# A pre-norm decoder layer on one core: z and h transposed by DMA instead of on TensorE, v and the cross attention as whole 128x128 products

## The reference

```python
x = x + attn(layernorm(x))            # causal, 16 heads of 16, W_qkv (768x256), W_out (256x256)
x = x + xattn(layernorm(x), ctx, mask)  # scores = q.ctx^T / 16, masked, softmax, times ctx
x = x + ffn(layernorm(x))

# ffn: two bit_linear layers round activations to 8 bits and weights to -1, 0, 1
def bit_linear(x, w, g):
    xn = x * rsqrt(mean(x * x) + 1e-5) * g
    s  = 127 / clip(max(abs(xn)), 1e-5);  xq = clip(round(xn * s), -128, 127) / s
    m  = 1 / clip(mean(abs(w)), 1e-5);    wq = clip(round(w * m), -1, 1) / m
    return xq @ wq.T
y = bit_linear(x, gate_w, gate_norm_w)        # 256 -> 1408
h = silu(y[:, :704]) * y[:, 704:]
out = bit_linear(h, down_w, down_norm_w)      # 704 -> 256
```

## Time and profile before

| | |
|---|---|
| time, median of 3 runs | 211.85 us (211.42 to 215.0) |
| the profiled execution | span 212.7 us from first to last instruction, 10882 instructions; no other time of it is given |
| busy share of the span | PE 91%, VectorE 78%, ScalarE 71%, GpSimd 64% |
| until the loop on PE begins | about 57 us |
| the loop, ten steps | about 57 to 169 us, 22.4 us for a turn of two steps |
| behind it | about 169 to 212.7 us |

### The profile page before, as it was taken

How to read it: one execution, slowest core, us unless ns; L and a number is a source line. 1 busy time by engine, 2 the same in 40 slices (tenths; PEclk the granted TensorE clock), 3 DMA queues, 4 the chain that set the end, 5 groups by cost and what they waited for, 6 DMA issues and landing times.

```text
span 212.7 us, 10882 instructions
## 1 busy us (share of the span) xinstructions
PE 194.6 (91%) x4104; PEld 153.5 (72%) x4107; DVE 165.7 (78%) x523; ACT 150.6 (71%) x422; POOL 137.1 (64%) x290
## 2 busy tenths in 40 slices
PE   4997999999999989999899989998999999889874
PEld 4785987978787868887787868787887866445532
DVE  1222587999988968798788888888879799999771
ACT  3468467767788886969587959887868866775821
POOL 4600341776758773948495857685755889999990
PEclk9998799999999999999999999999999999999999
DMA  5999000101010102020202011110101012000011
GB/s 172 379 330 348 25 3 6 52 3 51 6 49 30 53 6 74 0 76 2 76 0 74 2 28 48 32 44 25 51 25 51 24 52 77 0 5 26 2 43 59
DMA packets 11474, 12.79 MB, mean 60 GB/s; under 512 B 1009, under 2 KB 10801, under 8 KB 11442
## 3 DMA queue, kind: packets, MB, share of 16 engines
q1 hardware_dynamic: 11442, 12.41, 18.2%
HBM read 10.31 MB, written 2.10 MB: 58 GB/s over the span
## 4 chain that ended last, share of the span: by engine, by line
PE 72%; issue 10%; POOL 9%; DVE 4%; ACT 3%; DMA 1%; POOLq 0%; SPq 0%; DVEq 0%; ACTq 0%
PE ps L331 14%; PE ps L309 8%; PE ps L343 7%; PE ps L315 6%; PE ps L419 6%; PE ps L434 5%; PE ps L398 5%; PE ps L367 4%; PE ps L505 3%; PE ps L463 3%; POOL zh L1994 2%; PE ps L360 2%; PE ps L452 2%; PE ps L522 2%; PE ps L458 2%
## 5 line engine op out<-in xcount | busy, mean ns | idle before, releaser
L1994 POOL TENSOR_TENSOR zh<-hh,gd 128x352 f32<-128x352 f32 x32 | 31.2, 986 | 5.1 <-DVE hh L1331 4.7
L331 PE MATMUL ps<-yaT,wqk 128*128 128x128 f32 x256 | 32.9, 284 | 0.5 <-ACT yaT L681 0.5
L331 PEld LDWEIGHTS ps<-yaT,wqk 128*128 128x128 f32 x256 | 31.2, 199 | 1.2 <-ACT yaT L681 0.7
L1203 DVE TENSOR_REDUCE mx<-ps 128x16 f32<-128x1024 f32 x16 | 19.6, 1224 | 7.8 <-PE ps L367 7.6
L315 PE MATMUL ps<-wg,zT 128*128 128x352 bf16 x128 | 22.3, 312 | 0.5 <-ACT hT L681 0.4
L2016 POOL TENSOR_SCALAR hq<-zh,qh 128x704 f32<-128x704 f32 x16 | 13.6, 851 | 13.3 <-DVE qh L1360 13.0
L1910 POOL TENSOR_TENSOR rs<-ve,neghalf 128x1 f32<-128x1 f32 x32 | 20.2, 632 | 2.7
L681 ACT ACTIVATE hT<-ps 128x256 bf16<-128x256 bf16 (+1 forms) x32 | 15.5, 495 | 6.6 <-PE ps L309 6.5
L786 ACT ACTIVATE th_sb<-ps,th 128x352 f32<-128x352 f32 x32 | 17.4, 553 | 3.5 <-PE ps L315 1.8
L1318 DVE SCALAR_TENSOR_TENSOR th_sb<-th_sb,ps 128x352 f32<-128x352 f32 x32 | 16.4, 513 | 4.1 <-ACT th_sb L786 4.1
L738 ACT ACTIVATE pT<-ps 128x512 f32<-128x512 f32 x32 | 17.8, 609 | 1.3 <-PE ps L404 0.8
(11 more groups left out here) (120 smaller groups left out, 518.5 us busy)
## 6 DMA issues: line engine op xcount, KB each, us to landing
ct_in<-ctx_t SPq DMA_DIRECT2D x16, 128.0 KB, 2.1
cn_in<-ctx_n SPq DMA_DIRECT2D x16, 128.0 KB, 2.2
out<-o_out SPq DMA_DIRECT2D x16, 128.0 KB, 1.7
wg<-gate_t SPq DMA_DIRECT2D x1, 1408.0 KB, 7.7
x_in<-x SPq DMA_DIRECT2D x1, 1024.0 KB, 10.9
wd<-down_t SPq DMA_DIRECT2D x1, 640.0 KB, 8.7
wqk<-wqkv_t SPq DMA_DIRECT2D x1, 512.0 KB, 4.0
x_in<-x SPq DMA_DIRECT2D x1, 512.0 KB, 9.5
```

Of the source, the lines that this page charges most:

```text
L331: last = pe.matmul(qk_ps[:, e * P:(e + 1) * P], wqk[:, c, e * P:(e + 1) * P], yaT[:, t % 2, c, :], start=(c == 0), stop=(c == DC - 1))
L1203: V.tensor_reduce(out=mx[:, t % 2, :, 0, :], in_=scores, op=ALU.max, axis=AX).then_inc(ev["mx_d"], 1)
L1994: G.tensor_tensor(zh[:, t % 2, part], hh[:, t % 2, part], gd[:, part], ALU.mult).then_inc(ev[f"zh_d{j}"], 1)
```

## The change

v is projected by two products of 128x128 by 128x256, and ACT sorts the result into place with four copies instead of two. The cross attention scores of both sequences are made as one 128x128 block; the mask becomes two rows, one for each sequence, that also rule out the other sequence's 64 columns, and its product comes last instead of first. The weights `px` then need no 64x64 pieces: one transpose and one copy.

`zb` and `hb` are no longer transposed on PE: SP issues a transposing DMA from SBUF to SBUF for each, `zT` is its target and `hT` likewise, and `keep_zT`, `keep_hT_0`, `keep_hT_1` are gone from ACT. Rounding on POOL and bf16 on DVE stay as they are.

On PE the step now begins with `scores_q(s)` instead of ending with `scores_q(s+1)`; the mask part of the scores (`late_bf`) no longer waits for q and k; `scores_k` waits for the maxima only ahead of its last part; many waits for freed buffers are gone. The lists of all engines are in another order, and the first loads too. `keep_busy` has other counts: 16 ahead of `gate_up(14)`, 24 between `down(13)` and `down(14)`.

```diff
+            def transpose_z(t):                       # on SyncE
+                sp.wait_ge(ev["zb_d"], t + 1)
+                after(sp, ev["gu_ps0"], t - 1)
+                after(sp, ev["gu_ps1"], t - 1)
+                sp.dma_start_transpose(zT[:, t % 2, :, :], zb[:, t % 2, :]).then_inc(zT_ld[t % 2], 16)
+
+            def transpose_h(t):                       # on SyncE
+                sp.wait_ge(ev["hb_d"], t + 1)
...
+                after(sp, ev["d_ps"], t - 1)
+                sp.dma_start_transpose(hT[:, t % 2, :, :], hb[:, t % 2, :]).then_inc(hT_ld[t % 2], 16)
...
-                for b in range(2):                    # project_v
-                    for c in range(DC):
-                        for j in range(2):
-                            last = pe.matmul(v_ps[SEQ * j:SEQ * (j + 1), b * P:(b + 1) * P], yaT[:, t % 2, c, b * SEQ:(b + 1) * SEQ],
-                                             wv[:, c, j * P:(j + 1) * P], start=(c == 0), stop=(c == DC - 1))
+                for c in range(DC):
+                    last = pe.matmul(v_ps[:, :], yaT[:, t % 2, c, :], wv[:, c, :], start=(c == 0), stop=(c == DC - 1))
...
-                for rows in seqs:                     # cross_scores
-                    pe.matmul(sx_ps[rows, :], row_bf, mask_bf[:, t % 2, rows], start=True, stop=False)
-                for c in range(DC):
-                    for rows in seqs:
-                        last = pe.matmul(sx_ps[rows, :], yxT[:, t % 2, c, rows], ct_in[:, t % 2, c, rows], start=False, stop=(c == DC - 1))
+                for c in range(DC):
+                    pe.matmul(sx_ps, yxT[:, t % 2, c, :], ct_in[:, t % 2, c, :], start=(c == 0), stop=False)
+                pe.wait_ge(ev["mask_d"], at(t + 1))
+                pe.matmul(sx_ps, row_bf, mask_bf[:, t % 2, :], start=False, stop=True).then_inc(ev["sx_ps"], 1)
...
-                pe.wait_ge(ev["zT_d"], at(t + 1))     # gate_up_0, gate_up_1
+                pe.wait_ge(zT_ld[t % 2], loads(t, 16))
...
-                pe.wait_ge(ev["hT_d0"], at(t + 1))    # down
-                pe.wait_ge(ev["hT_d1"], at(t + 1))
+                pe.wait_ge(hT_ld[t % 2], loads(t, 16))
...
-                for j in range(2):                    # keep_v
-                    rows = slice(SEQ * j, SEQ * (j + 1))
-                    last = copy(v2[rows, t % 2, :, :, j, 0:DK], v_ps[rows, :].rearrange("p (b i d) -> p b i d", b=2, i=PAIRS))
+                for b in range(2):
+                    for j in range(2):
+                        last = copy(v2[SEQ * j:SEQ * (j + 1), t % 2, b, :, j, 0:DK],
+                                    v_ps[SEQ * b:SEQ * (b + 1), j * P:(j + 1) * P].rearrange("p (i d) -> p i d", i=PAIRS))
```

More of the change, by code:

```diff
@@ L282, in at, with loads @@
                 return kept[t.base]
-            def loads(t):
-                return 32 * (t // 2 + 1) if isinstance(t, int) else pe.snap(t.turn * 32 + 32 * (t.base // 2 + 1))
+            def loads(t, each):
+                return each * (t // 2 + 1) if isinstance(t, int) else pe.snap(t.turn * each + each * (t.base // 2 + 1))
             def within(t, least, most):
@@ L408, in readout @@
             def readout(t, *users):
-                columns = SEQ if isinstance(t, int) else 32
+                columns = SEQ if isinstance(t, int) and t < FIRST else 32
                 pe.wait_ge(ev["v_d"], at(t + 1))
@@ L542, in _ @@
[L542 to L543 removed]
+            project_v(2)
+            scores_q(2, ("exp_d1", 2))
+            readout(1)
+            transpose_ya(3)
+            project_out(0)
             weight_totals(("mx_d", 3))
[L545 to L547 removed]
             project_qk(3, ("oN_d", 2))
[L549 removed]
@@ L550, in _ @@
-            cross_scores(0, ("v_d", 3))
-            project_out(1, ("oT_d", 2))
-            scores_q(3, ("exp_d0", 3), ("exp_d1", 3))
-            transpose_cross_weights(0, ("x1_d", 2))
-            transpose_ya(4, ("yxT_d", 1))
-            readout(2, ("q_d", 4), ("k0_d", 4), ("k1_d", 4))
-            project_v(3, ("expx_d", 1))
-            transpose_max(3, ("mx_d", 4))
-            cross_readout(0, ("pxT_d", 1))
-            transpose_yx(1, ("yaT_d", 5))
+            transpose_max(2)
+            transpose_readout(1)
@@ L560, in _ @@
+            scores_k(2, ("mT_d", 3))
+            transpose_yx(0)
+            project_out(1)
+            transpose_ya(4, ("yxT_d", 1))
+            cross_scores(0)
+            scores_q(3, ("exp_d0", 3))
+            readout(2)
+            transpose_cross_weights(0)
+            project_v(3)
+            cross_readout(0)
+            transpose_max(3)
+            transpose_yx(1)
             project_qk(4, ("oN_d", 3))
             transpose_readout(2, ("x2_d", 1))
-            cross_scores(1, ("v_d", 4))
@@ L572, in _ @@
-            gate_up_1(0, ("mx_d", 5))
+            scores_q(4, ("exp_d1", 4))
+            readout(3)
+            cross_readout(1)
             gate_up_0(0, ("mx_d", 5))
+            gate_up_1(0)
             transpose_readout(3, ("x2_d", 2))
-            project_qk(5, ("oN_d", 4))
-            transpose_max(4, ("h1_d0", 1))
-            transpose_yx(2, ("zT_d", 1))
-            project_out(3, ("oT_d", 4))
-            cross_scores(2, ("v_d", 5))
-            scores_k(4, ("hh_d0", 1), ("h1_d1", 1), ("hh_d1", 1), ("mT_d", 5))
+            project_qk(5)
@@ L1800, in _ @@
+            residual_1(14)
             gated_1(11)
@@ L2281 @@
     small[:, B_ID:B_ID + P] = np.eye(P)
-    small[0, B_ROW:B_ALL] = 1
+    for b in range(2):
+        small[b, B_ROW + SEQ * b:B_ROW + SEQ * (b + 1)] = 1
     for j in range(2):
@@ L2294 @@
     wv = wqkv[:, 2 * D:].reshape(D, PAIRS, 2, DK).transpose(0, 2, 1, 3).reshape(D, D)
+    mask = np.asarray(inputs["mask_BxS2_bk0"]).reshape(tiles, 2, SEQ)
+    own = np.zeros((2, tiles, P), mask.dtype)
+    for b in range(2):
+        own[b, :, SEQ * b:SEQ * (b + 1)] = mask[:, b]
     arrays = {
```

1253 lines of the change are left out of this document (595 added, 658 removed).

## The result

| | before | after |
|---|---|---|
| time, median | 211.63 us of 4 runs (211.03 to 215.0) | 219.43 us of 4 runs (217.01 to 223.35) |
| profiled execution | span 212.7 us | 219.03 us, span 217.2 us |

A kernel's executions are not all alike, and every ratio here leaves out those more than 1.5% above their kernel's fastest. The ratio is 1.032, 95% interval 1.027 to 1.037. The change makes the kernel slower by 3.2%. I had forecast 1.4% faster.

The account below looks back on a forecast made before the run. PE was taken to bound the loop, each tile's feed-forward chain the stretch behind it. Terms: -4.3 + 0.6 in the loop, -1.0 ahead, +1.8 behind, -2.9 us in all, giving 209.0 us; whole range 204.5 to 223.

Parts of the forecast that it names:

- the term ahead of the loop: Ahead of the loop: two pairs of z transposes go and PE waits less; -1.0 us, bounds +1 and -3.
- Behind the loop: Behind the loop: PE's shorter list gains nothing, last z and h landings come later; +1.8 us, bounds +0.5 and +4.
- some 3 us: Context loads go out a step later, still some 3 us ahead of `cross_scores` beyond their 2.2.
- In the loop: Ten loop steps: -4.3 us from PE's shorter list, +0.6 for late h landings of tiles 2 and 6.
- Removed transposes: PE's list in each loop step: zb transposes gone -0.21 us, six of seven hb transposes gone -0.34 us.
- my VectorE rival: In the loop VectorE takes over as the bound, a turn stays at 22.5 us; 213.5 us total, chance 0.19.
- the cross scores' +0.12 a step: Cross scores on PE: four 128-column passes plus mask take 0.53 us instead of 0.41; bounds 0 and +0.15.
- the gap goes: Rival: the loop branch hides behind `down`, five gaps of 0.75 us go; 204.3 us total, chance 0.14.
- The landings: Transposing DMAs land in 2.3 us for z and 3.0 for h; low bounds 1.7 and 2.2, far 3.0 and 4.7.
- their covers: Time before PE needs a landing in the loop: z 2.85 us; h 2.7 to about 4.1 us by tile.
- The term that I called the most fragile, h's: h's transposing DMA lands in 3.0 us; over about 3.7 us the loop's gain is gone. Late-h rival: 222.5 us, chance 0.20.
- the whole sum off the median: The sum of -2.9 us was taken off the median of 211.85 us, giving 209.0; the profiled span was 212.7.

Follow-up runs that it names:

- Run 11: Changed kernel, but ahead of and behind the loop in before's order (SyncE's first loads kept), transposes behind the loop on TensorE: 213.6 us, ratio 1.008.
- run 13: Kernel before with whole 128x128 products for v and cross attention, and one 1 MB load of x held until the first readout: 216.5 us, ratio 1.023.
- run 5: Changed kernel with, ahead of the loop, the weight-sum product and both VectorE gate-weight passes later and the first x1 variance earlier: 217.5 us.
- run 2: Kernel before with z and h transposed by DMA in the changed kernel's SyncE order, nothing else changed: 221.4 us, ratio 1.045.
- run 8: Kernel before with only h transposed by DMA, z left on TensorE: 213.6 us, ratio 1.010.
- run 6: Changed kernel with the context loads of tiles 5 to 15 one step earlier in SyncE's queue: 219.9 us, ratio 1.040.
- run 4: Kernel before with both DMA transposes of z and h and whole products for v and cross attention, in before's order: 229.6 us, ratio 1.086.
- run 3: Kernel before with whole 128x128 products for v and cross attention, all else unchanged: 217.55 us, ratio 1.018.
- run 12: Run 11 with the half-width products of the kernel before for v and cross attention: 211.5 us, ratio 0.994.
- run 7: Kernel before with the loop's branch moved to right behind down, instruction order on every engine unchanged: 211.1 us, ratio 0.998.
- run 10: Changed kernel with only the transposes behind the loop back on TensorE, in before's order and fillers there: 220.4 us, ratio 1.037.
- run 15: Run 12 with the 1 MB load of x held until the first readout and context loads one step earlier: 211.96 us, ratio 0.990.
- the first profile: Kernel before, unchanged, as first profiled for the prediction: span 212.7 us.
- the typical one: Kernel before, unchanged, profiled once more: 211.5 us, span 209.6 us.

## Why the prediction was wrong

**The step that failed is the term ahead of the loop, "I take -1.0 of the 6.0 idle us; bounds +1 and -3".** It was +7.2. I had counted two pairs of transposes and left the rewritten order of five engines uncosted, because "PE waits less for q, k and the maxima". Run 11 splits it: 5.0 us for the order, 1.8 for the first z's landings and the order of the loads (run 11 against the 56.0 of run 13), 0.4 for whole products. Part of the order's cost is that ScalarE's |wg| pass and VectorE's two passes over the gate weights stand where PE, and GpSimd through its slowed instructions, had to wait for them: run 5, which moved the product of the sums and both VectorE passes, won 2.0 of the 5.0. The other 3.0 lie on the way to the first zb, and no run took them apart. All of this is in the order of instructions, which can be read beforehand: which instruction of 1.6 or 2.5 us stands ahead of one that PE needs. The slowed GpSimd instruction too stood in the trace of before (2.02 us at 41.94).

**Behind the loop** the mechanism was right and the size off: +4.1 for +1.8, just over my bound of +4. I had counted the last z and the last h only. There PE waited for four landings of z and two of h, 2.3 and 1.4 us in all; in the old order the same transposes cost 10.1 us, 7.7 of it z's (runs 2 and 8). The context load adds 1.2 (run 6), which I had said had "some 3 us" to spare: so it has in the loop, not behind it, where SyncE's queue waits for zb. The new order behind the loop gives 7.1 of run 4's loss back.

**In the loop** -3.7 was right by luck, from the wrong terms. Removed transposes gave 1.5 us and not 4.9 (run 2). Two things are in that. PE's list got shorter by 0.43 us a step and not by 0.55: in the step at 112 us of both profiles `gate_up` to `down` takes 7.28 us for 7.61, and `down` to `readout` without its gap 1.56 for 1.66, so the transposes of zb are worth 0.10 where I had read 0.21. And PE's idle time rose by 1.5 us, in waits for VectorE and ScalarE; that was my VectorE rival, which I gave 0.19. Whole products cost 1.7, where the cross scores' +0.12 a step makes 1.1 (run 3), and in the new order perhaps nothing (97.1 beside run 12's 96.9). The new order with its branch behind `down` gives 4.4 (run 4 against the changed kernel), which I had at nothing. The branch alone is 0.7 of it (run 7), so my rival "the gap goes" has the right event and about a fifth of its price.

**The landings** of 2.3 and 3.0 us were 2.3 and 2.7, and their covers held: PE's waits for hT in the loop are under 0.3 us. The term that I called the most fragile, h's, was sound. Four z transposes of 16 landed late, at 4.0, 3.4, 3.0 and 2.8 us, and PE waited 1.09 and 0.66 us for the first two of these. The latest of them, in the list of queues from 58.7 to 63 us:

```profile
q8 instruction: 1, 0.02, 1.8%
...
zT<-zb SPq DMA_TRANSPOSE x1, 4.0
```

It landed 1.2 us behind the end of that 16 KB packet. Ahead of the loop this is the rule: in the changed kernel and in runs 5, 6, 10, 11, 12 and 15 PE waits 0.7 us or more for zT eleven times, and all but one of these waits end 1.1 to 1.3 us behind the end of such a packet. That the packet delays the landing is not tested, but much of the 1.8 us above may be that.

**The base** has a share in the first point. Against the first profile the stretch ahead is +4.4, against the typical one +7.2. I took the whole sum off the median, though its -1.0 ahead was to come from idle time and a slow stretch that only the long, profiled execution had; I had noted that its span was over the median, and drew nothing from it.

What stays open: what makes the first instruction packet early or late, and why a stall or a late landing follows some of the packets and not others. Whether the two stalls behind the loop in run 10 belong to that program or to chance was not tried. What the GpSimd slowdown alone costs the changed kernel was not tested either; run 5 moved both passes and the product of the sums at once.

## What to carry to other kernels

Cost a reordering by stretches, and the stretches without a steady state first: in the loop the forecast held, by luck, and 11 us were lost in the 105 us around it, where no other work covers a landing or a long pass over weights. An engine that is busy 97% of a loop (PE here) may still be worth only a few tenths a step, if the next engine is that close; shortening its list needs a new order of the others as well. Take two profiles of the kernel before, or check its span against the median of the times, before a stretch of it is called typical.
